# Routing each token of a mixture-of-experts FFN through its own expert only, by token queues in DRAM with weights fetched per tile

## What is computed

```python
x = x + xattn(layernorm(x), ctx)          # 16 heads of 16; block pattern; out @ Wo.T
xf = layernorm(x)
top1 = argmax(softmax(xf @ gate_w.T))
masked = xf[None] * one_hot(top1).T[:, :, None]
h = relu(einsum('end,edh->enh', masked, w1) + b1[:, None])
routing_output = (einsum('enh,ehd->end', h, w2) + b2[:, None]).sum(0)
shared = relu(xf @ sw1 + sb1) @ sw2 + sb2
x = x + routing_output + shared           # hidden width 1024
```

## Time and profile before

| | us |
|---|---|
| median of 3 runs | 1029.99 (1029.34 to 1030.01) |
| span of the profiled execution | 1025.1 |
| PE busy | 971.3, 95% |
| DVE busy | 655.2, 64% |
| ACT busy | 526.8, 51% |
| POOL busy | 464.9, 45% |
| mean granted clock of PE | 0.972 |

### The profile page before, as it was taken

The page is one execution under the profiler, slowest core; times in us unless marked ns, Lnnn a source line. Parts: engine busy times, 40 slices in busy tenths (PEclk is TensorE's granted clock), DMA queues, the critical chain, the costliest instruction groups (busy, mean ns, idle before and its releaser), DMA issues.

```text
span 1025.1 us, 24123 instructions
## 1 busy us (share of the span) xinstructions
PE 971.3 (95%) x8864; PEld 848.3 (83%) x8864; DVE 655.2 (64%) x1074; ACT 526.8 (51%) x1197; POOL 464.9 (45%) x561
## 2 busy tenths in 40 slices
PE   3576999999999999999999999999999999999998
PEld 2346889798988979798897979889797988979788
DVE  4674566676666677566767766666776666676640
ACT  3253555546455555645555564545546454554544
POOL 7454436262443627244362724426272542726254
PEclk8586999999999999999999999999999999999999
DMA  9654261422626142262624226252422526240000
GB/s 247 159 128 75 62 85 46 69 48 61 92 61 82 57 62 44 65 89 61 82 65 56 43 71 82 61 82 72 51 44 73 78 61 86 68 57 20 17 12 11
DMA packets 72564, 71.40 MB, mean 70 GB/s; under 512 B 6224, under 2 KB 70352, under 8 KB 72544
## 3 DMA queue, kind: packets, MB, share of 16 engines
q1 hardware_dynamic: 70624, 64.83, 34.2%
q0 software_dynamic: 1920, 6.29, 2.2%
HBM read 48.03 MB, written 23.07 MB: 69 GB/s over the span
## 4 chain that ended last, share of the span: by engine, by line
PE 84%; DMA 7%; DVE 5%; POOL 1%; SPq 1%; issue 1%; ACT 1%; DVEq 0%; ACTq 0%; POOLq 0%
PE hid L349 26%; PE acc L491 25%; PE nd L416 12%; PE work L401 7%; PE work L386 5%; PE work L349 4%; DMA QP<-scratch_m 2%; PE work L444 2%; DMA scratch_m<-mT 2%; DVE xhat L717 2%; PE work L430 1%; DVE nmax L740 1%; DMA h<-w 1%; DMA QP<-scratch_q 1%; PE work L454 1%
## 5 line engine op out<-in xcount | busy, mean ns | idle before, releaser
L900 POOL TENSOR_TENSOR hl<-h,hh 128x256 fp32r<-128x256 f32 x384 | 284.8, 750 | 504.0 <-ACT hh L626 503.9
L626 ACT ACTIVATE h<-hid,bias 128x256 f32<-128x256 f32 x384 | 183.1, 477 | 295.8 <-PE hid L349 228.5
L746 DVE RECIPROCAL T<-nd 128x256 f32<-128x256 f32 x128 | 224.5, 1754 | 111.2 <-PE nd L416 111.2
L349 PE MATMUL hid<-X,w_hi 128*128 128x256 f32 x1536 | 289.1, 286 | 0.7 <-DVE X L697 0.7
L349 PEld LDWEIGHTS hid<-X,w_hi 128*128 128x128 f32 x1536 | 240.1, 189 | 26.8 <-issue 21.5
L349 PE MATMUL hid<-X,w_lo 128*128 128x256 f32 x768 | 216.3, 282 | 0.0
L491 PE MATMUL acc<-w_hi,hh 128*128 128x256 f32 x768 | 195.5, 288 | 0.0
L491 PE MATMUL acc<-w_lo,hh 128*128 128x256 f32 x768 | 189.1, 280 | 0.0
L740 DVE TENSOR_REDUCE nmax<-work 128x8 f32<-128x512 f32 x256 | 162.5, 682 | 39.2 <-PE work L386 38.3
L626 ACT ACTIVATE hh<-hid,bias 128x256 fp32r<-128x256 f32 x384 | 183.6, 478 | 0.0
L615 ACT ACTIVATE PT<-work 128x512 f32<-128x512 f32 x256 | 139.5, 604 | 67.9 <-PE work L401 67.9
(11 more groups left out here) (118 smaller groups left out, 1071.9 us busy)
## 6 DMA issues: line engine op xcount, KB each, us to landing
KP<-scratch_k SPq DMA_DIRECT2D x96, 128.0 KB, 4.9
QP<-scratch_q SPq DMA_DIRECT2D x96, 128.0 KB, 8.3
scratch_k<-T SPq DMA_DIRECT2D x16, 512.0 KB, 3.0
scratch_q<-T SPq DMA_DIRECT2D x16, 512.0 KB, 3.5
xin<-x SPq DMA_DIRECT2D x16, 256.0 KB, 9.6
ctx_in<-ctxT SPq DMA_DIRECT2D x16, 256.0 KB, 9.4
x<-x SPq DMA_DIRECT2D x16, 256.0 KB, 3.7
out<-x1b SPq DMA_DIRECT2D x16, 256.0 KB, 2.2
```

Source lines behind the costliest of these rows:

```text
L349: mm = nc.tensor.matmul(dst, R(s), R(m), start=n == 0, stop=n == len(steps) - 1)
L626: last = nc.scalar.activation(dst, hid[:, u % 2, a, :], ACT.Relu, bias=bias1[:, k:k + 1])
L746: nc.vector.reciprocal(T[:, p, :], nd[:, p % 2, 1, :]).then_inc(sem["inverted"], 1)
L900: nc.gpsimd.tensor_tensor(R(hl[:, u % 2, a]), h32[:, u % 2, a], hh[:, u % 2, a], ALU.subtract).then_inc(sem["hl_done"], 1)
```

## The change

The mask goes. After its second layernorm each token is one row of 260 floats (`rows`: 256 values and its number), and POOL scatters the rows of a sequence into one DRAM array, `queue`, with two indirect DMAs (`append`): tokens of expert 1 from the front, tokens of expert 2 from the back. The places come from a count of the gate's choices (`counts` on PE, `route` on DVE, `update` on POOL). In each iteration POOL then picks a full tile of 256 rows of one expert (`select`) and leaves its start and its expert in `control`. SP reads the start and loads the tile (`load_tile`). ACT reads the expert and fetches that expert's weights, four DMAs of 1 MB (`load_weights`), from `wx` in DRAM, where the split weights were kept in iterations 0 and 1. The tile goes through 4 units. The constant of the other expert is added (`idle_sel`, `finish_routed`), and POOL adds the rows to the output in DRAM by their numbers (`add_routed`, two indirect accumulating DMAs), after the sequence's shared part was stored there.

An iteration has 8 units (4 routed, 4 shared) where it had 12. The shared part starts in iteration 1, the routed part in iteration 3. There are 17 routed tiles: 15 full ones and one with what is left of each expert. Units in all: 17 x 4 + 16 x 4 = 132, before 16 x 12 = 192; of these 20, less one up, come after iteration 15. Layernorm, split and gate of sequence `i - 1` move from the end of iteration `i - 1` to the scores of iteration `i`. The loop now covers iterations 3 to 14.

```diff
-SCORE_STEPS = ((0,), (1, 2, 3), (4, 5, 6), (7, 8), (9, 10), (11, 12, 13), (14, 15))
-PAIR_UP = {0: 6, 3: 7, 6: 8}
-PAIR_DOWN = {1: 5, 4: 6, 7: 7}
+SCORE_STEPS = ((0,), (1, 2, 3), (4, 5), (6, 7, 8), (9, 10), (11, 12, 13), (14, 15))
+PAIR_UP = {3: 6, 6: 7}
+PAIR_DOWN = {1: 4, 4: 5}
+ROUTED_T_PAIR = 5
...
+            def load_tile(i):
+
+                before, appended, last = held(sp, sp_counts, i - 2, 32 * i, i - 1)
+                if type(i) is int and i > BATCH:
+                    appended = 32 * BATCH
+                sp.wait_ge(sem["ident_loaded"], 16)
+                sp.wait_ge(sem["sel_done"], last)
+                sp.wait_ge(sem["rows_out"], appended)
+                if type(i) is not int or i > 2:
+                    sp.wait_ge(sem["rT_full"], before)
+                    sp.wait_ge(sem["ids_done"], before)
+                start = sp.value_load(control[0:1, 0:1], min_val=0, max_val=QROWS - TILE)
+                sp.dma_start(rowin[:, :, :], queue[bass.ds(start, TILE), :].rearrange("(t p) w -> p t w", p=P)) \
+                    .then_inc(sem["row_loaded"], 16)
+
+            def iteration(i, more, loads=True):
                 shift(i)
                 if more:
                     bounces(i + 1)
-                if ffn:
+                if type(i) is not int or i >= 2:
+                    load_tile(i)
+                if type(i) is not int or i >= 1:
...
+                    if step == 2 and present(("x2T", 0), i):
+                        shared_tokens(i)
+                    if step % 2 == 0 and step < 6:
                         up(step // 2 + 1)
-                    else:
+                    elif step < 6:
                         down(step // 2)
+                if present(("cnt", 0), i):
+                    counts(i)
                 maxima(i)
-                down(3)
...
+                up(4)
                 if more:
                     front_xT(i + 1)
-                up(5)
+                down(3)
                 if more:
                     front_project(i + 1, "k", 1, c_hi, c_lo, "c_lo")
                     front_project(i + 1, "q", 0, a_hi, a_lo, "xT_lo")
-                down(4)
-                if not more:
-                    up(6)
...
-                scores_t(i, 0, more)
-                scores_t(i, 1, more)
+                up(5)
+                scores_t(i, 0)
+                scores_t(i, 1)
...
-                up(9)
-                down(8)
-                attention_out(i, more)
-                up(10)
-                project_out(i, more)
-                down(9)
-                up(11)
-                down(10)
-                prep_tokens(i, more)
+                    if p == ROUTED_T_PAIR and present(("rT", 0), i):
+                        routed_tokens(i)
+                down(6)
+                attention_out(i)
+                up(0, i + 1)
+                project_out(i)
+                down(7)
                 if more:
                     front_v(i + 1)
-                down(11)
...
+            def load_weights(i):
+
+                selected, = held(act, act_counts, i - 1)
+                act.wait_ge(sem["proj_lo"], 4)
+                act.wait_ge(sem["sel_done"], selected)
+                if type(i) is int and i == 2:
+                    act.wait_ge(sem["wx_stored"], 16 * (PIECES - SHARED_PIECES))
+                expert = act.value_load(control[0:1, 1:2], min_val=0, max_val=1)
+                for k in range(RU):
+                    if type(i) is not int or i > 2:
+                        act.wait_ge(sem["w2_done"], unit_no(i, k) + 1)
+                    act.dma_start(WR[:, k].rearrange("p a b c -> p (a b c)"),
+                                  wx[bass.ds(expert * P, P), k].rearrange("p a b c -> p (a b c)")) \
+                        .then_inc(sem[f"wr_loaded{k}"], 16)
...
+                relu(i, 5)
+                if type(i) is not int or i >= 2:
+                    load_weights(i)
+                if type(i) is int and i == 0:
+                    act.wait_ge(sem["proj_lo"], 4)
                 exps(i, 0)
                 exps(i, 1)
...
+            def iteration(i, more):
+                later = present(("x2T", 0), i)
+                maximum(i, 0)
+                maximum(i, 1)
+                slot(i, 0)
+                if later:
+                    norm2_apply(i - 1)
+                for j in range(2, 6):
+                    maximum(i, j)
+                slot(i, 1)
+                if later:
+                    shared_low(i - 1)
+                for j in range(6, 9):
+                    maximum(i, j)
+                slot(i, 2)
+                if later:
+                    gate_scores(i - 1, 0)
+                maximum(i, 9)
+                maximum(i, 10)
+                if later:
+                    gate_scores(i - 1, 1)
+                    choose(i - 1)
+                slot(i, 3)
+                for j in range(11, 14):
+                    maximum(i, j)
+                if more:
+                    norm1_stats(i + 1)
+                maximum(i, 14)
+                maximum(i, 15)
                 if more:
                     norm1_apply(i + 1)
                 low(i, "mT_hi", work[:, BANK[("mT", 0)], 0:P], mT[:, 0, :], mT[:, 1, :], "m_lo")
+                if later:
+                    route(i - 1)
+                slot(i, 4)
+                if type(i) is int and i == 1:
+                    dve.wait_ge(sem["c_full"], 1)
...
+            def append(b):
...
+                here, tiles = held(pool, pool_counts, b + 1, 16 * (b - 1))
+                pool.wait_ge(sem["zeroed"], 3)
+                if type(b) is not int or b > 1:
+                    pool.wait_ge(sem["row_loaded"], tiles)
+                pool.wait_ge(sem["id_done"], here)
+                pool.wait_ge(sem["ln2_done"], here)
+                pool.wait_ge(sem["pos_done"], here)
+                for t in range(TT):
+                    pool.indirect_dma_start(queue[:, :], by_row(ap=pos[:, t:t + 1], axis=0), rows[:, t, :], None) \
+                        .then_inc(sem["rows_out"], 16)
...
+                if more:
+                    reciprocal_deviation(i + 1, 0)
+                    context_low(i + 1)
+                if later:
+                    append(i - 1)
+                hidden_low(i, 4)
+                slot(i, 4)
+                if later:
+                    update(i - 1)
+                if type(i) is not int or i >= 2:
+                    select(i - 1)
+                hidden_low(i, 5)
+                if active(i, 0):
...
+                ffn_up(i, k)
+                ffn_down(i, k - 1)
+                if k == UNITS - 2:
+                    pe.wait_ge(sem["row_loaded"], 16 * LAST)
+                    transposed(work[:, 2], rowin).then_inc(sem["rT_full"], 1)
+            i = LAST + 2
+            for k in range(UNITS):
+                ffn_up(i, k)
+                ffn_down(*((i, k - 1) if k else (i - 1, UNITS - 1)))
+                if k == RU - 2:
+                    pe.wait_ge(sem["x2_lo"], BATCH)
+                    pe.wait_ge(sem["left_masked"], 1)
+                    transposed(work[:, 0], xhat).then_inc(sem["rT_full"], 1)
+                if k == RU:
+                    pe.wait_ge(sem["cnt_copied"], BATCH)
+                    pe.wait_ge(sem["left_masked"], 2)
+                    transposed(work[:, 1], xin).then_inc(sem["rT_full"], 1)
+            i = LAST + 3
+            for k in range(RU):
+                ffn_up(i, k)
+                ffn_down(*((i, k - 1) if k else (i - 1, UNITS - 1)))
+            ffn_down(i, RU - 1)
```

1035 lines of the change are left out of this document (707 added, 328 removed).

## The result

The changed kernel takes 1184.5 us (1182.8 to 1187.5, four runs) beside 1030.0 for the kernel before: 1.150 of it, with a 95% interval of 1.147 to 1.153. The forecast was 1085, its range ended at 1135. The sign was right, the size was not: +15%, where I had worked out +5%.

What follows compares the result with a forecast made beforehand. PE's list was taken to bound the kernel before the change, with much saved work becoming idle PE time. 1025.1 - 5 + 3.6 + 29 + 27.5 = 1080, plus 4.9 outside the span: 1085 us, range 1030 to 1135.

Steps and rivals of the forecast that it cites:

- the out stretch: Last transposed scores to next first score: 19.5 becomes 14.7 us, set by the DMA landing of K and Q.
- Scores, 17.4: First score to maxima: 13.7 becomes 17.4 us, because DVE's list grows by layernorm, gate and choice.
- Maxima to values, 13.5: Maxima to first values: 10.5 becomes 13.5 us, with ACT's relus, register load and weight issues ahead of the exps.
- With small waits 7.8: Within maxima to values: PE's list ahead of unit 5's relus takes 7.8 us.
- this ends at 9.3, level with the relus: Within maxima to values: POOL's choice of a tile ends 9.3 us behind the maxima, when unit 5's relus end.
- Values, 16.2: First values to last transposed scores: 15.7 becomes 16.2 us, with as many ups and downs on PE as before.
- PE's clock falls at the wait for the exps: Rival, chance 0.18: idling 4 us per iteration lowers PE's clock, +2 to +4 us per iteration, 1109 to 1133 us.
- The rival of POOL's late queue: Chance 0.10: POOL's indirect issues wait for DVE work beside them, +3 us per iteration, 1121 us.
- The rival of PE as the bound: Chance 0.07: PE's list stays the bound, an iteration takes 48.5 to 54 us, time 925 to 991 us.
- The prologue and iteration 0, -5: Start of the kernel: iteration 0 gets 5 us shorter, as fewer pieces are split there and the last loads go.
- The tail, 122.5 behind the first score: From iteration 15's first score to the end: 122.5 us, +27.5, with 4 us of waits for tiles.
- PE busy "730 to 780": Sign to look for: PE's busy time falls to some 730 to 780 us, about 70%.

Runs made afterwards that it cites:

- c_gate_back: Changed kernel with layernorm, gate and choice of a sequence moved back to the end of its own iteration on DVE; 1153.5 us, ratio 1.120.
- a_warm: Changed kernel with PE kept busy by extra matmuls in its two waits of each iteration; 1151.3 us, ratio 1.121.
- n_unit4_early: The kernel of m with unit 4's up moved ahead of the transpose of the maxima; 1005.5 us, ratio 0.977.
- m: Changed kernel reordered: SP issues weights, layernorm at iteration's end, tail edits, exps before relus, spread in halves, gate and choice behind next maxima; 1015.7 us, 0.986.
- i: Changed kernel with weights issued by SP, layernorm and gate at iteration's end, tail edits, and first two exps before unit 5's relus; 1045.2 us, 1.016.
- h_prologue: Changed kernel with the prologue's seventh to tenth piece loads held back until the first spread of K and Q landed; 1179.8 us, ratio 1.143.
- d_tail: Changed kernel, tail alone: last tiles get their own token numbers, last tile loaded before the last shared part is stored; 1165.6 us, ratio 1.133.

## Why the prediction was wrong

The sum against the profiled execution was 1080, the span 1185.6. The 105.5 between them lie as follows. Up to the maxima of iteration 3: 243.7, forecast 229.5 - 5 + 3.6 = 228.1, 15.6 short. The twelve distances of the loop: 796.9, forecast 743.3 (714.3 and 29), 53.6 short. Behind the last maxima: 145.0 against 106.0, 39.0 short. Less 2.7, because I had counted the longer scores of iteration 15 twice.

**What bounds the kernel, and the direction: right.** PE's work went and became waits. `spread` behind the last transposed scores bounds the out stretch: 15.0, forecast 14.7; with it in halves 12.6, PE's list (I had put that 2 us under). **Scores, 17.4: right**, 17.9, and shown by c_gate_back; at full clock (a_warm) it is 17.3.

**Maxima to values, 13.5: mis-sized**, 15.5. The exps waited for the register load and the issues, as the forecast had it. "With small waits 7.8", PE's list ahead of unit 5's relus, failed by the clock: it ran at 0.66 and 0.86, and the first transposed scores came at 9.6; a_warm has them at 8.0. But a_warm still has 15.0 for the stretch, so 1.5 of the 2.0 would have come at full clock too. The step behind them is "this ends at 9.3, level with the relus". POOL's choice ends at 10.6, with the clock up or not. The indirect issues were shorter than the 1.16 written; the twelve small operations with their waits took 3.9 instead of 2.9, and the append began 0.3 later. Behind `control` the register load took 0.8 (taken 1.1) and the issues 2.2 on average (taken 1.8). These add up to the 1.5 that a_warm lies above the forecast. No run made POOL's choice shorter alone. The Trainium skill, "Runtime: NRT & Kernel Launch", "The ~15µs preamble/postamble breakdown", has about 1.3 us for a register load in the preamble, of several registers; 0.8 was measured for one here.

**Values, 16.2, "Nothing is saved here": it lost 1.8**, again by the clock. a_warm gives 16.3.

So the main step that failed in the loop, 3.1 of the 4.7 us by which an iteration is longer than forecast, is the weight of the rival "PE's clock falls at the wait for the exps". It had 0.18 and +2 to +4 per iteration; it came true in the loop, with a price inside its own range. Against it I held that "in rows 2 nothing shows a fall"; but in rows 2 PE never waits, so they could not. A forecast that makes PE idle 4 us in each iteration has to put the clock in its sum and not among the rivals. I also missed the second place, the wait for the maxima: if DVE sets the scores stretch, as the forecast says, PE has small gaps all along it. The other 1.6 are POOL's choice and the issues. The Trainium skill, "TensorE: Matmul & The Clock Gate", "HAM oscillation — how this bites in real kernels", describes that a kernel which idles in each round starts each burst cold; the trace agrees, with 0.50 in the window 525 to 529.

**The rival of POOL's late queue: did not come.** The indirect issues took 1.0 and 1.6 us with little spread (0.98 to 1.10 and 1.56 to 1.68 over all 64). In this kernel they hardly meet DVE work, so the rival's condition was seldom there. In n_unit4_early 26 of the 32 accumulating ones stand beside 0.6 us or more of DVE work each (nearly all of it divisions) and take 1.61 us on average, no more. `control` was late all the same, by the small operations. The Trainium skill, "SBUF — State Buffer", "SBUF: two separate sides", tells of DMAs held up several times over beside a copy on DVE; no issue of this kernel shows it.

**The rival of PE as the bound: not reached.** n_unit4_early comes to 55.1, under the 57.1 from which it decides, and the time goes under that of the kernel before. PE is idle in it for 155 us. The point of decision was near: m at 55.6 and n at 55.1 are faster, i at 56.7 is not yet. By m's own ends the time of the kernel before is reached at 56.8, by i's at 55.4. That this lies so near 57.1 is partly luck, as two errors work against each other in m: its tail is 22 longer than forecast, and its first three iterations are 7 shorter.

**The prologue and iteration 0, -5: wrong sign**, by 11; the other 4.5 of the 15.6 lie in iterations 1 and 2. The first maxima came at 53.5 instead of 45.0. The first score is 4.9 late, perhaps in part by the piece loads beside the first spread (h_prologue); the other 3.6 lie in the scores, where splits and sums of pieces stand among the maxima. I had counted the buffers that no longer wait, and what DVE does between the divisions, but not what it does between the first maxima.

**The tail, 122.5 behind the first score, with 4 us for tile waits: mis-sized**, 39 short. 18.1 are three waits: for `hidden_low` behind the append and the choice on POOL (3.7), the last tile (6.9), the token numbers (7.6). Their price in the sum was "none to 10", bounded by a landing that I took from POOL's direct DMAs; beside the weights these took 9 to 10 each, and they follow each other. The ending has 15 instead of 6.5, most of it POOL's closing `DRAIN` of 7.6 us, for which the sum has no term. Of what is left, 5.3 lie in iteration 15 (14.5 to the values and 18.5 for them, where 11.5 and 16.2 were written), whose exps still waited for the weights, and some 4 are half clock behind the waits, by d_tail. About 7 I have not taken apart. I had set 130 us as the sign of a wrong tail, and 162 followed the last iteration's first score.

**PE busy "730 to 780": wrong by its own arithmetic.** 60 units at 2.84 from 971 leave 801; with the transposes and the start of each train after a wait it is 851 in the best version, and 917 here, with half-rate work in it.

**Smaller terms.** The 4.9 us outside the span set the runs' median against the span of one execution; where a run has both numbers, 1.8 to 2.0 lie outside. The weights were to end at 27; the prediction's own 12.2 and 12.7 give 24.9, and 27.1 behind the maxima was measured. And the spread's rows moved at 115 GB/s from 493 to 507 in the kernel before, not at 125.

## What to carry to other kernels

The work taken from the saturated engine was worth nothing here until the waits that it had covered were found. Write them down as a new timeline, the small operations of the slowest helper engine too, and where that timeline shows the matmul engine idle, price the half clock behind it in the sum, not among the risks. Fetching parameters per tile cost little by its bytes and much by its place: ahead of the exps on ACT the register load and the issues cost 66 us, the clock's part included, and later, just before another transfer that the next stage waits for, the bytes cost 67. In a tail, look for buffers whose reuse waits for the landing of a DMA, because no other work hides them there.

## What the runs showed that I had not expected

An indirect DMA with accumulation takes 1.60 us to issue on POOL, one that stores 1.04; once the weights beside it are gone it lands in 4.1 us, where it had seemed to need 10. The closing `DRAIN` on POOL takes 7.4 to 7.6 us in this program, with the last two indirect DMAs or without them, and 2.8 in the kernel before; it stands in no row of busy time. And 880 useless matmuls made the kernel 33 us faster.
